# Moving normalization, statistics and transposes within the last tile of a batch in a fused transformer kernel (one core)

## The reference

```python
x = x + 0.5 * ffn(layernorm(x))      # DEPTH = 2 layers
x = x + attn(layernorm(x))           # the middle part, a fast-weight memory
x = x + 0.5 * ffn(layernorm(x))      # the same 2 layers again
```

```python
h = shift_token(x)                   # second half of the columns is the row before's
q, k, v = split(h @ wqkv)            # 8 heads of 64
q, k = rotary_xpos(l2norm(q) * qs, l2norm(k) * ksc)
x = x + local_attention(q, k, v) @ wo     # window of 128 rows
h = shift_token(x)
h = (h - mean(h)) / sqrt(var(h) + 1e-5) * lg + lb
a, g = split(h @ w1 + b1)
x = x + (a * gelu(g)) @ w2 + b2
```

## Time and profile before

| | |
|---|---|
| median of 3 runs | 2677.72 us |
| lowest and highest | 2675.68 and 2679.54 us |
| the profiled execution | 2677.72 us |
| its span, first to last instruction | 2675.8 us |
| TensorE, VectorE, ScalarE, GpSimd busy | 94, 75, 68 and 58% |

### The profile page before, as it was taken

How to read it: one execution, slowest core, us unless ns; L and a number is a source line. 1 busy time by engine, 2 the same in 40 slices (tenths; PEclk the granted TensorE clock), 3 DMA queues, 4 the chain that set the end, 5 groups by cost and what they waited for, 6 DMA issues and landing times.

```text
span 2675.8 us, 79930 instructions
## 1 busy us (share of the span) xinstructions
PE 2513.4 (94%) x29664; PEld 2230.6 (83%) x29664; DVE 1996.2 (75%) x6533; ACT 1818.2 (68%) x5192; POOL 1551.1 (58%) x1767
## 2 busy tenths in 40 slices
PE   8899999999999999999999899999999999999998
PEld 7788888888888888888777788888888888888888
DVE  7777777777777777777655777777777777877776
ACT  5777777666776776666454777766667677767675
POOL 6556666556656665665213566656656666656654
PEclk9999999999999999999999999999999999999999
DMA  3122011003000000005101000000003100000000
GB/s 120 33 81 74 20 46 53 26 21 115 14 2 3 2 2 26 2 2 184 49 18 33 2 2 2 2 2 2 2 2 116 34 2 18 18 18 18 17 18 26
DMA packets 75954, 82.18 MB, mean 31 GB/s; under 512 B 37552, under 2 KB 61872, under 8 KB 74416
## 3 DMA queue, kind: packets, MB, share of 16 engines
q1 hardware_dynamic: 70176, 75.51, 8.5%
q10 hardware_dynamic: 5392, 1.56, 0.2%
HBM read 49.53 MB, written 26.74 MB: 29 GB/s over the span
## 4 chain that ended last, share of the span: by engine, by line
PE 41%; DVE 24%; POOL 13%; issue 9%; ACT 8%; DMA 3%; SPq 1%; DVEq 0%; ACTq 0%; POOLq 0%
PE bank L1125 6%; POOL pr L634 6%; PE bank L1127 6%; PE bank L1126 6%; PE bank L1359 5%; DVE pr L1728 4%; PE bank L1188 3%; DMA stt<-stt 3%; DVE t L1691 3%; DVE t L1694 3%; PE bank L1161 3%; ACT pr L821 3%; POOL r L618 3%; PE bank L1236 2%; PE bank L1524 2%
## 5 line engine op out<-in xcount | busy, mean ns | idle before, releaser
L634 POOL TENSOR_TENSOR pr<-pr,rden 128x384 f32<-128x384 f32 (+1 forms) x512 | 436.2, 859 | 456.9 <-DVE rden L1737 456.2
L821 ACT ACTIVATE pr<-pr,nb 128x192 f32<-128x192 f32 (+1 forms) x1024 | 438.3, 431 | 162.3 <-DVE nb L1728 162.2
L1125 PE MATMUL bank<-h2T,w 128*128 128x256 f32 x1408 | 405.6, 288 | 44.5 <-issue 31.4
L1126 PE MATMUL bank<-h2T,w 128*128 128x256 f32 x1408 | 395.3, 281 | 0.0
L1127 PE MATMUL bank<-h2T,w 128*128 128x256 f32 x1408 | 395.2, 281 | 0.0
L1728 DVE CUSTOM_DVE_ANT_0 pr<-bank,maskb,r 128x192 f32<-128x192 f32 (+1 forms) x1024 | 352.3, 395 | 37.2 <-issue 26.0
L666 POOL TENSOR_TENSOR uTl<-t,uTh 128x256 fp32r<-128x256 f32 x288 | 218.9, 760 | 207.4 <-ACT uTh L921 206.6
L1825 DVE SCALAR_TENSOR_TENSOR t<-bank,b,t 128x256 f32<-128x256 f32 (+1 forms) x384 | 183.5, 480 | 176.1 <-ACT t L906 104.2
L1125 PEld LDWEIGHTS bank<-h2T,w 128*128 128x128 f32 x1408 | 266.6, 189 | 56.9 <-issue 35.8
L1125 PE MATMUL bank<-wqkv,hT 128*128 128x512 f32 x768 | 306.9, 400 | 4.6 <-DVE nb L1728 3.9
L1126 PE MATMUL bank<-wqkv,hT 128*128 128x512 f32 x768 | 302.6, 394 | 0.0
(11 more groups left out here) (244 smaller groups left out, 7048.3 us busy)
## 6 DMA issues: line engine op xcount, KB each, us to landing
wqkv<-wqkv_split SPq DMA_DIRECT2D x18, 512.0 KB, 6.2
w<-w_split SPq DMA_DIRECT2D x3, 2816.0 KB, 9.9
Y<-in_x SPq DMA_DIRECT2D x8, 512.0 KB, 7.3
out<-Y SPq DMA_DIRECT2D x8, 512.0 KB, 3.9
stt<-stt SPq DMA_DIRECT2D x224, 3.0 KB
h<-out SPq DMA_DIRECT2D x7, 512.0 KB, 4.0
out<-h SPq DMA_DIRECT2D x7, 512.0 KB, 3.0
stt<-stt SPq DMA_DIRECT2D x192, 0.0 KB
```

Of the source, the lines that this page charges most:

```text
L634: e.tensor_tensor(probs(j, t), probs(j, t), rden[:, 2 * j:2 * j + 2].unsqueeze(2).to_broadcast([P, 2, w]), ALU.mult).then_inc(pn_done, 1)
L821: last = e.activation(probs(j, t)[:, g, :], probs(j, t)[:, g, :], ACT.Exp, bias=nb[:, hd:hd + 1], scale=-1.0, accum_out=den[:, hd:hd + 1])
L1125: e.matmul(out, left[0], right[0], start=first, stop=False)
L1126: e.matmul(out, left[0], right[1], start=False, stop=False)
```

## The change

Four lists are changed; no instruction is added or taken away.
- SP: `load_wqkv(L + 1)` is issued after `move_stats` of tile 1 and not before it.
- ScalarE, step 3: the copy of `H2T(0)` is done before the two copies of `A2` of the tile ahead.
- TensorE, step 3: `fill(2)`, then `H2T(0)`, then `WO(3)`; before it was `WO(3)`, `H2T(0)`, `fill(2)`.
- VectorE, step 3: `halves(2)` moves from behind `LN_moments(0)` to behind the two `O_add` of tile 3, and `LN_apply(0)` moves ahead of these.

```diff
@@ sync: sequence @@
                 move_stats(L, b, 0, st_moved[0])
+                move_stats(L, b, 1, st_moved[0])
                 if last and L + 1 < LAYERS:
                     load_wqkv(L + 1)
-                move_stats(L, b, 1, st_moved[0])
                 move_stats(L, b, 2, st_moved[1])
@@ scalar: sequence @@
                     if t == 3:
                         O_first(L, b, t)
                         O(L, b, t)
+                        H2T(L, b, 0)
                     if ahead:
                         A2(*ahead)
-                    if t == 3:
-                        H2T(L, b, 0)
@@ tensor: sequence @@
                     if ahead:
                         A2(*ahead, 0)
                         A2(*ahead, 1)
+                    fill(2)
                     if t == 3:
+                        H2T(L, b, 0)
                         WO(L, b, t)
-                        H2T(L, b, 0)
-                    fill(2)
@@ vector: sequence @@
                         if t == 3:
                             LN_moments(L, b, 0)
-                            halves(L, b, t - 1)
                         squares(idx(*ahead), 1)
...
                         if not ahead:
                             WO(L, b, t - 1)
                             LN_moments(L, b, 0)
-                            halves(L, b, t - 1)
...
                     if t == 3:
+                        LN_apply(L, b, 0)
                         for i in pair:
                             O_add(L, b, t, i)
+                        halves(L, b, t - 1)
                         O(L, b, t)
-                        LN_apply(L, b, 0)
                         if prev:
                             W2(*prev, t)
                         H2T(L, b, 0)
```

## The result

| | before | after |
|---|---|---|
| median | 2676.7 us (2672.7 to 2679.5, four runs) | 2786.7 us (2785.9 to 2788.8, four runs) |
| span of the profiled execution | 2675.8 us | 2785.8 us |

The ratio is 1.041 (1.040 to 1.043): the change made the kernel 110 us slower. The forecast was 2785 us, slower. One execution of e1 (3395 us) and one of the kernel before in the first group (2870 us) ran at a mean granted clock of 0.65 and 0.82 and enter no ratio.

The account below looks back on a forecast made before the run. TensorE was busy 94% of the span, with VectorE's chain through `WO(3)` setting each batch's end. Ordinary batches 53, last batches 1, layer 0 28, weights 17 and clock 8 made 107 us: 2785 us, range 2750 to 2822.

Parts of the forecast that it names:

- The mechanism, ordinary batches: VectorE, step 3: tile 2's statistics land 4.8 us behind the late `halves(2)`, so `WO(3)` stalls at `tile2_told`: 53 us.
- The rival "faster": Tile 2's DMAs told within 2.5 us of `halves(2)`, so `WO(3)` 0.6 us earlier in 30 batches: 2660 us, chance 0.05.
- the lower bound for it: GpSimd's power might shorten from 1.46 us towards 1.02, taking up to 0.44 us off the 2.3 us delay.
- Its size per batch: Delay of `WO(3)` and the chain behind it: 2.3 us in each of 23 batches, bounds 1.6 to 2.5.
- TensorE and ScalarE: Step 3 reordering starts W1 some 0.6 us earlier, worth that only if VectorE's chain moves along.
- Layer 0: Batches 0 to 6: late weights delay ScalarE's `next_hi`, table load and DMA; 4.0 us in place of 2.3, 28 us.
- The weights: Ends of layers 0 and 2: the later `load_wqkv` makes VectorE wait for the table of rotations, 8.5 us each, 17 us.
- The clock: TensorE idles some 3 us around `H2T(1)`, so its clock may fall to 1.2 GHz: 8 us, of 0 to 51.
- The row with 1.32 us of work at full clock: Profile stretch of 3.4 us near the end, before the change, whose little work left the clock at 1.00.
- The one with 1.56: Profile stretch after the start, before the change: 1.56 us of work in 3.4, then clock 0.51 for 3.4 us.
- The rival "in every batch": The clock falls in every batch, 51 us in place of 8: 2828 us, chance 0.10.
- the two last batches: Last batches of the two passes, with no tile ahead: 0.5 us each, 1 us for two (0 to 4).

Follow-up runs that it names:

- e1: The changed kernel with `halves(2)` put back behind `LN_moments(0)`, all other moves kept: 2675.9 us, ratio 1.000 to the kernel before.
- the first group: The follow-up runs e1 to e4, timed beside the kernel before, whose median there was 2675.9 us (13 runs).
- e7: The changed kernel with a semaphore of their own for tile 2's five DMAs and VectorE's wait for them moved behind `halves(3)`: 2707.9 us, ratio 1.011.
- e9: The kernel before with only TensorE's and ScalarE's new order of step 3, VectorE and SP untouched: 2652.5 us, ratio 0.991.
- e3: The changed kernel with both `halves(2)` and `load_wqkv` put back, so only TensorE's and ScalarE's order and the early `LN_apply(0)` remain: 2657.2 us, ratio 0.993.
- e8: The changed kernel with SP's load of the next layer's weights (layer 0, batches 0 to 6) put ahead of `move_stats(2)`: 2781.8 us, ratio 1.038.
- e2: The changed kernel with `load_wqkv` put back ahead of `move_stats(1)`: 2766.0 us, ratio 1.034 to the kernel before.
- e5: The kernel before with `load_wqkv` alone moved behind `move_stats(1)`: 2697.6 us, ratio 1.007.
- e4: The changed kernel with 14 unread products added on TensorE where it waits for `H2T(1)`: 2768.8 us, ratio 1.034 to the kernel before.

## Why the prediction was right

**The mechanism, ordinary batches: right.** The step was that `tile2_told` becomes the last wait at 4.8 us behind `halves(2)`. It measured 4.81 us in the batch of the sums, and `WO(3)` is 2.2 us later against GpSimd's power (7.17 less 5.00), where 2.3 was predicted. e1 takes the late `halves(2)` away and the whole cost goes. e7 leaves it late and takes away what is queued behind the wait; the ordinary batches' cost goes as well. The rival "faster" needed a landing in 2.5 us, and the chain shows SP's queue alone above that, with 3.14 us ahead of the fifth issue. GpSimd's power stayed at 1.46 us, so the lower bound for it didn't come.

**Its size per batch: 1.8 to 2.0 and not 2.3 us,** within its bounds of 1.6 and 2.5. In layer 1, batch 2, 14.67 us passed before between the power and the end of VectorE's part of `H2T(1)`, and 16.44 after, 1.8 more. What was gained back lies behind `WO(3)`. The chain before, in the same batch:

```profile
863.23 0.88 DVE h L1807
...
864.15 0.34 PE bank L1281
```

The first row is the third instruction of `LN_apply(2)`. It took 0.8 to 0.9 us in 12 of the 32 batches before, and 0.33 or 0.34 in all but one after. A part of this was lost again in the transposes behind it, which end 0.38 us behind `LN_apply(2)` here and 0.54 after, at the lower clock. Why the instruction was slower before wasn't tried.

**TensorE and ScalarE: right, and worth more than it got.** Against the power W1 began 0.7 us earlier (4.48 and not 5.18 us behind it), where 0.6 was predicted, and TensorE's wait for `oT` went. The prediction gave that gain nothing, as the chain behind it moved the other way. By itself it is 23 us (e9), or 18.7 with `LN_apply(0)` ahead (e3). The rival "faster" had 18 for it.

**Layer 0: the step failed, and 3.1 and not 4.0 us.** The prediction put ScalarE's DMA behind `next_hi` and the table load. The trace of after has it issued at 332.23, at the start of `next_hi`. The table load then holds only the first Gelu, and with it U. That explains why the wait of VectorE at the moments is there 25 times and not 32: the seven without it are these batches, in which the DMA was told before VectorE came. In e8 it is there 31 times. The right part was that ScalarE waits for the weights; e8 took that wait away, but of the 18.6 us in the lengths only 4.7 went with it, and the 2.3 us a batch that stay are of the size of the late chain in the other batches.

**The weights: right in mechanism, a little small in size.** 17 us predicted (13 to 18), measured 20.7 in e2, 18.3 in e5, 18.7 from e1 and e3, and 18.3 in the lengths (11.4 + 12.8, less twice the 2.96 of an ordinary batch). Layer 0, batch 7, after: SP's queue, and VectorE:

```profile
633.04 3.16 SPq L426 DMA_DIRECT2D wqkv<-wqkv_split  x6
636.24 0.47 SPq L428 DMA_DIRECT2D rot<-rot_scaled  x1
```
```profile
645.34 0.69 DVE L1690 TENSOR_TENSOR t<-bank,rot 128x512 f32<-128x512 f32 x1 [8.20 <-DMA rot<-rot_scaled]
```

The table lands 12.3 us behind the first issue, and VectorE waits 8.2 us (9.7 in layer 2). The prediction had 8.5 for both. TensorE also waits for the pieces that `A1` needs, 4.2 us, ahead of that and not on top of it. The rule from the Trainium skill, "DMA: Bandwidth & Descriptors", Rules for kernel authors, issue a DMA early and wait late, holds in both of its places: 110.8 us for tile 2's statistics and 18 to 21 us for the weights.

**The clock: the term that was mis-sized, at least some 17 us and not 8.** The granted clock in stretches of 3.4 us, layer 1, batch 2, after (busy time of PE, PEld, DVE, ACT, POOL, then the clock):

```profile
900.10:903.50 3.40, 1.27 (x11) 1.03 (x9) 2.31 (x10) 1.21 (x4) 1.58 (x2) 1.00 0.01 0
903.50:906.90 3.40, 3.40 (x16) 3.22 (x16) 1.95 (x6) 1.31 (x4) 1.57 (x2) 0.51 0.01 2
```

TensorE worked 1.27 us in 3.4, then had 0.51 of its clock (1.2 GHz) for 3.4 us, just when the second half of W1 began. The clock was at that level in 32 stretches, 116 us together, against 2 and 6 us before. Of the 32 batches 22 have such a stretch at this place, 11 to 13 us behind the first product of `H2T(0)`; in layer 0 it is rare there. The row with 1.32 us of work at full clock, near the end, on which I leaned, misled me. The one with 1.56 was the better guide. The rival "in every batch" was nearly true in number and not in price: it had 1.7 us for a fall, and e4 shows 0.9 to 1.0 in an ordinary batch, 17.9 us together. At half the clock for 3.4 us TensorE could lose 1.7, but part of that time it waits anyway. With the gap filled in e4, 23 of the 32 falls are gone. The prediction should have priced it per batch.

**The sum.** Chain in all batches: 82 predicted, and at most some 71 by the experiments (110.0 less 20.7 less 17.9). Weights 17, and 20.7. Clock 8, and 17.9 at least. 107 and 110: two errors of some 10 us cancelled. That was luck, and the time came out better than its parts. The starts and ends of the passes have 8.0 us in the lengths, where 1 was predicted for the two last batches. The step itself came there: in layer 3, batch 7, `WO(3)` began 5.55 us behind the first `O_add` before (2646.91 less 2641.36) and 6.01 after (2756.22 less 2750.21), 0.5 more. Where the rest of the 8.0 comes from wasn't tried. The lower bounds without the clock add up to 73 us and not to 74 as the prediction has it; the range that begins at 2750 goes by 73.

## What to carry to other kernels

A wait costs what is queued behind it on its engine, not what it waits for: moving the wait behind `WO(3)` and `halves(3)`, for which a semaphore more was enough (e7), gave back three quarters of 110 us, with the DMAs as late as before. When several orders are changed in one edit, run the parts alone: here 23 us to be won lay beneath 133 us of loss. And price a new gap on TensorE twice, once as idle time and once as the lower clock behind it.

## What the runs showed of the hardware that was not expected

- Five small DMAs from SP, 0.64 to 0.85 us of its queue each, were told 4.81 us behind the instruction that released them. Of this 3.14 us passed before the fifth was issued.
- ScalarE's queue issued a DMA at 332.23 while the engine began a copy of 0.63 us and, behind it, loaded a table for 1.28 us. So it was in all seven batches of its kind: the order in the list doesn't put the DMA behind the end of what stands ahead of it.
- A fall of the granted clock came at the same place in 22 of 32 batches, and TensorE's single wait before it, at `H2T(1)`, was 2.7 us at the longest. Fourteen unread products a batch took the stretches at the lower clock from 32 to 9.
